# First attention with one exponential pass per four groups, and the change from feed-forward to second attention written out

## What is computed

```python
h = take_along(x, top_k(x @ w + b, 179))            # 179 of 256 tokens are kept
# layer 0: additive attention, 12 heads of 16
q, k, v = heads(ln(h) @ Wq.T + bq), heads(ln(h) @ Wk.T + bk), heads(ln(h) @ Wv.T + bv)
score = einsum('bhtsd,d->bhts', tanh(q[:, :, :, None, :] + k[:, :, None, :, :]), ws) + bs
h = h + (softmax(score) @ v) @ Wo.T + bo
h = h + quantized_ffn(ln(h))                         # 192 -> 768 -> 192, gelu
# layer 1: x is quantized with one scale for the whole tensor
xq = fake_quant(ln(h), scale = max(abs(ln(h))) / 127)
h = h + attention(xq)                                # power-of-two softmax
h = h + mixture_of_16_experts(ln(h))                 # one expert per token
```

## Time and profile before

| | |
|---|---|
| median of 3 runs | 1449.03 us (1444.05 to 1456.63) |
| the profiled execution | 1448.74 us, of which the span from first to last instruction is 1446.8 us |
| busy: PE, DVE, ACT, POOL | 1153.0, 1105.7, 1003.6, 861.9 us |
| DMA | 103.06 MB, most of it in the first 250 us |

### The profile page before, as it was taken

The page is one execution under the profiler, slowest core; times in us unless marked ns, Lnnn a source line. Parts: engine busy times, 40 slices in busy tenths (PEclk is TensorE's granted clock), DMA queues, the critical chain, the costliest instruction groups (busy, mean ns, idle before and its releaser), DMA issues. The chain is left out here.

```text
span 1446.8 us, 39002 instructions
## 1 busy us (share of the span) xinstructions
PE 1153.0 (80%) x16164; PEld 874.5 (60%) x16164; DVE 1105.7 (76%) x2109; ACT 1003.6 (69%) x921; POOL 861.9 (60%) x978
## 2 busy tenths in 40 slices
PE   4766898788778887887788779847999999989496
PEld 3544665566556655665566458835667666767396
DVE  8797998899889998998899867753566677665443
ACT  1389999999999999999999967732234433433142
POOL 4098878887888788888888977540012222123354
PEclk9899999999999999999999999975899999988698
DMA  9999997000000000000000002000000100010352
GB/s 254 360 360 356 352 344 246 2 2 2 2 2 2 2 2 2 2 3 2 1 2 2 2 15 53 0 1 1 2 2 12 59 17 15 12 39 9 94 152 65
DMA packets 75449, 103.06 MB, mean 71 GB/s; under 512 B 6303, under 2 KB 73640, under 8 KB 75282
## 3 DMA queue, kind: packets, MB, share of 16 engines
q1 hardware_dynamic: 63784, 87.90, 18.5%
q10 hardware_dynamic: 6860, 6.12, 1.6%
q0 software_dynamic: 4640, 6.65, 1.4%
HBM read 18.32 MB, written 83.85 MB: 71 GB/s over the span
## 5 line engine op out<-in xcount | busy, mean ns | idle before, releaser
L917 ACT ACTIVATE work<-work 128x2864 f32<-128x2864 f32 (+1 forms) x272 | 688.8, 2578 | 32.2 <-DVE work L436 31.3
L436 POOL TENSOR_TENSOR work<-shared 128x1253 f32<-128x1253 f32 (+1 forms) x272 | 613.5, 2267 | 151.6 <-PE psum L1789 117.8
L1789 PE MATMUL psum<-work,ws_place 128*32 128x179 f32 x8640 | 397.6, 325 | 165.8 <-ACT work L917 165.6
L436 DVE TENSOR_TENSOR work<-psum,shared 128x1611 f32<-128x1611 f32 (+3 forms) x288 | 486.5, 1722 | 0.6
L1789 PEld LDWEIGHTS psum<-work,ws_place 128*32 128x32 f32 x8640 | 261.7, 112 | 274.4 <-ACT work L917 214.2
L1979 PE MATMUL psum<-shared 32*64 32x179 f32 (+1 forms) x1728 | 142.5, 367 | 8.1 <-DVE shared L1497 8.1
L756 POOL TENSOR_TENSOR tsum<-tstats 128x4 f32<-128x4 f32 (+1 forms) x16 | 3.7, 233 | 200.8 <-DVE tstats L1414 200.8
L1276 DVE SCALAR_TENSOR_TENSOR p_sb<-psum,bs_col,s_top 128x358 f32<-128x358 f32 x144 | 82.1, 570 | 43.9 <-PE psum L1802 30.7
L1979 PEld LDWEIGHTS psum<-shared 32*64 32x64 f32 (+1 forms) x1728 | 81.1, 159 | 56.5 <-issue 36.5
L1503 DVE TENSOR_SCALAR pt_region<-pt_region 128x1074 uint32<-128x1074 uint32 x48 | 34.6, 721 | 98.4 <-ACT pt_region L988 98.4
L906 ACT ACTIVATE pt_region<-psum,bs_neg 128x512 f32<-128x512 f32 x144 | 95.3, 663 | 1.6 <-PE psum L1802 1.5
(11 more groups left out here) (365 smaller groups left out, 1984.2 us busy)
## 6 DMA issues: line engine op xcount, KB each, us to landing
xs_dram<-pad_row SPq DMA_DIRECT2D x23, 3088.0 KB, 27.6
pt_region<-xs_dram ACTq DMA_DIRECT2D x19, 193.0 KB, 2.6
pt_region<-xs_dram SPq DMA_DIRECT2D x19, 193.0 KB, 2.4
xs_dram<-pad_row SPq DMA_DIRECT2D x1, 2895.0 KB, 27.0
work<-in_x SPq DMA_DIRECT2D x2, 768.0 KB, 10.1
work<-in_x ACTq DMA_DIRECT2D x2, 768.0 KB, 16.2
work<-in_L_ffn_W2T SPq DMA_DIRECT2D x1, 1536.0 KB
work<-in_L_ffn_W1T SPq DMA_DIRECT2D x1, 1536.0 KB
```

The lines of the kernel that those rows point to most:

```text
L436: ins = eng.tensor_tensor(dst[:, a * KEEP:e * KEEP].rearrange("p (u s) -> p u s", s=KEEP), k[:, h * KP:h * KP + KEEP].unsqueeze(1).to_broa ...
L917: act.activation(a, a, ACT.Tanh).then_inc(tanh_done, 1)
L1789: ins = pe.matmul(bank_s[p % 2][32 * quad:32 * quad + 32, at:at + KEEP], ws_place[:, j, :], arg_slot(n)[:, u * KEEP:(u + 1) * KEEP], start ...
```

## The change

In the first attention `p_sb` holds the two groups of a duo 192 columns apart instead of 179, so 3 transposes of 128 take the place of 4 (2 for the last duo, as before). The three pieces are then: keys 0 to 127 of the even group; keys 128 to 178 of the even group and 0 to 63 of the odd group; keys 64 to 178 of the odd group. ACT takes the exponential of two banks, so of two duos (four groups), in one instruction of 128x768, after the tanh of groups 8, 12 and 16 and of groups 2 and (the single last group) 4 of the next batch: 5 passes a batch for 9. Duo k goes to bank k modulo 2, and PE may turn into it only once the pass over the pair before is done; duo 8 is turned at group 3 for group 2. Odd groups meet V in another order of rows, so SP copies V of each batch by three DMAs to `v_extra`, which PE waits for before the context; the context is made for even and odd groups apart, with 32 products of 96 columns and 32 of 48. SP issues two fills behind each batch's copies, until the 24 are out, instead of all at the start.

The last steps of DVE's feed-forward are written out: other order, the means of batches 14 and 15 by DVE and not POOL, with the additions of 14 and 15 ahead of them. The maximum over the partitions is a transpose on PE and a reduction on DVE. PE does 20 idle products instead of 12, not before `norm_max(12)` is done, and the transpose of the maximum stands behind them. The first batch's q, k and v go to four PSUM banks, without waits between. Two semaphores are merged into others, and two blanks are added on POOL at the start.

```diff
-        pt = [pt_region[:, 2 * n * PT_COLS:2 * (n + 1) * PT_COLS].rearrange("p (s c) -> p s c", s=2) for n in range(2)]
+        pt = [pt_region[:, 2 * n * PT_COLS:2 * n * PT_COLS + 3 * DUOS * 128].rearrange("p (s k c) -> p s k c", s=3, k=DUOS) for n in range(2)]
+        v_extra = [pt_region[:, 2 * n * PT_COLS + 3 * DUOS * 128:2 * n * PT_COLS + 3 * DUOS * 128 + 2 * HEADS * VC].rearrange(
+            "p (s h v) -> p s h v", s=2, h=HEADS) for n in range(2)]
...
-        p_sb = [sb(f"p_sb{n}", [128, KEEP + WIDE]) for n in range(2)]
+        p_sb = [sb(f"p_sb{n}", [128, 2 * ROW]) for n in range(2)]
...
+        def qkv_bank(c, fill):
+
+            if isinstance(c, int) and c == 0:
+                return (bank_pre, bank_out, bank_s1, bank_pta)[fill]
+            return bank_out if fill else bank_pre
+
...
-            for lo in range(0, XS_ROWS, 2048):
-                n = min(2048, XS_ROWS - lo) // 128
-                sp.dma_start(xs_dram[lo:lo + 128 * n, :].rearrange("(j p) d -> p j d", p=128),
-                             pad_row[:, :].unsqueeze(1).to_broadcast([128, n, RW])).then_inc(e_zeroed, 16)
+
+            def fill(n):
+
+                lo = 2048 * n
+                rows = min(2048, XS_ROWS - lo) // 128
+                sp.dma_start(xs_dram[lo:lo + 128 * rows, :].rearrange("(j p) d -> p j d", p=128),
+                             pad_row[:, :].unsqueeze(1).to_broadcast([128, rows, RW])).then_inc(e_zeroed, 16)
+
+            FILLS = -(-XS_ROWS // 2048)
+            for b in range(B):
+                n, v = b % 2, v_sb[b % 2]
+                sp.wait_ge(v_ready, b + 1)
+                need(sp, v_spread[n], 48 * (b // 2))
+                sp.dma_start(v_extra[n][HALF_K:128, 0, :, :], v[0:HALF_K, 0, :, :]).then_inc(v_spread[n], 16)
+                sp.dma_start(v_extra[n][0:HALF_K, 1, :, :], v[HALF_K:128, 0, :, :]).then_inc(v_spread[n], 16)
+                sp.dma_start(v_extra[n][HALF_K:LAST_K, 1, :, :], v[0:TB, 1, :, :]).then_inc(v_spread[n], 16)
+                for k in range(2 * b, min(2 * b + 2, FILLS)):
+                    fill(k)
...
-            with pool.Fori(0, B // 2) as j:
+            with pool.Fori(0, B // 2 - 1) as j:
                 pair_norms(j, 0)
-            pool.wait_ge(x_maxed, 1)
-            pool.partition_all_reduce(x_allmax[:, :], x_max[:, :], 128, RMAX).then_inc(x_alled, 1)
             pool.wait_ge(f_added, B)
...
-            def exps(b, k):
-
-                p, w = b * DUOS + k, duo(k)
-                if k == 0:
+            def exps(b, q):
+
+                if q == 0:
                     need(act, ctx_psum, 2 * b - 2)
-                act.wait_ge(turned, p + 1)
-                act.activation(pt[b % 2][:, :, 256 * k:256 * k + 128 * w],
-                               bank_pt[p % 2].rearrange("p (s c) -> p s c", s=2)[:, :, 0:128 * w],
-                               ACT.Exp, bias=bs_neg[:, :], scale=1.0).then_inc(exp_done, 1)
+                act.wait_ge(turned, b * DUOS + min(2 * q + 2, DUOS))
+                if q < EXPS - 1:
+                    banks = psum[:, 4 * 512:6 * 512].rearrange("p (k c) -> p k c", k=2)[:, :, 0:384].rearrange("p k (s c) -> p k s c", s=3)
+                    ins = act.activation(pt[b % 2][:, :, 2 * q:2 * q + 2, :].rearrange("p s k c -> p k s c"), banks,
+                                         ACT.Exp, bias=bs_neg[:, :], scale=1.0)
+                else:
+                    ins = act.activation(pt[b % 2][:, 0:2, 2 * q, :], bank_pta[:, 0:256].rearrange("p (s c) -> p s c", s=2),
+                                         ACT.Exp, bias=bs_neg[:, :], scale=1.0)
+                ins.then_inc(exp_done, 1)
             for b in range(B + 1):
...
-                    if g % 2 and g >= 7 and real(b):
-                        exps(b, (g - 7) // 2)
-                    if g in (0, 2, 3, 4) and real(b - 1):
-                        exps(b - 1, DUOS - 4 + (0, 2, 3, 4).index(g))
+                    if g in (8, 12, 16) and real(b):
+                        exps(b, (g - 8) // 4)
+                    if g in (2, 4) and real(b - 1):
+                        exps(b - 1, 2 + g // 2)
...
-                dve.scalar_tensor_tensor(p_sb[p % 2][:, 0:w * KEEP].rearrange("p (a s) -> p a s", s=KEEP), s, bs_col[:, :],
+                dve.scalar_tensor_tensor(p_sb[p % 2][:, 0:w * ROW].rearrange("p (a s) -> p a s", s=ROW)[:, :, 0:KEEP], s, bs_col[:, :],
...
+            def last_stats(n):
+
+                dve.wait_ge(f_added, B - 1 + n)
+                for t, rows in TILES:
+                    ins = dve.bn_stats(stats[0:rows, 2 + 2 * n + t, :], resid[0:rows, B - 1 + n, t, :])
+                rlink(ins)
...
+            def last_pair():
+
+                cols = slice(2, 6)
...
+                rlink(dve.tensor_tensor(v, vE, vO, ALU.add))
+                dve.tensor_scalar(m, m, 0.5, None, ALU.mult)
+                dve.tensor_scalar(v, v, 1.0 / D, EPS, ALU.mult, ALU.add)
+                rlink(dve.scalar_tensor_tensor(d, d, 0.25, d, ALU.mult, ALU.mult))
+                rlink(dve.tensor_tensor(v, v, d, ALU.add))
+                dve.tensor_scalar(h, v, -0.5, None, ALU.mult)
+                rlink(dve.tensor_copy(g, v.bitcast(I32)))
+                rlink(dve.tensor_scalar(g, g, -0.5, 1597463007.0, ALU.mult, ALU.add))
+                rlink(dve.tensor_copy(y.bitcast(I32), g))
+                for n in range(3):
+                    rlink(dve.tensor_tensor(s, y, y, ALU.mult))
+                    rlink(dve.tensor_tensor(s, s, h, ALU.mult))
+                    rlink(dve.scalar_tensor_tensor(y, s, 1.5, y, ALU.add, ALU.mult))
...
+            staged(dve, ffn_step, (2, 5), closed=True)
+            ffn_add(B - 4)
+            hidden_round(B - 3, 1)
+            dve.wait_ge(f_added, B - 3)
+            dve.wait_ge(stats_taken, B - 4)
+            pair_tile_stats(B - 3, 0)
+            norm_max(B - 7, 1)
+            ffn_add(B - 3)
+            hidden_round(B - 2, 0)
+            dve.wait_ge(f_added, B - 2)
+            pair_tile_stats(B - 2, 1)
+            norm_max(B - 6, 0)
+            norm_max(B - 5, 1)
+            ffn_add(B - 2)
+            hidden_round(B - 1, 1)
+            last_stats(0)
+            ffn_add(B - 1)
+            last_stats(1)
+            last_pair()
+            for b in range(B - 4, B):
+                norm_max(b, b % 2)
...
             dve.wait_ge(x_alled, 1)
+            dve.tensor_reduce(x_allmax[:, :], bank_k0[:, 0:128], AX.X, ALU.max).then_inc(x3_step, 1)
+            dve.wait_ge(x3_step, 1)
             dve.tensor_scalar(x_scale[:, :], x_allmax[:, :], 1.0 / 127.0, 1e-8, ALU.mult, ALU.max).then_inc(x3_step, 1)
...
-                bank, src = bank_pt[p % 2], p_sb[p % 2]
+                bank, src = bank_pt[k % 2], p_sb[p % 2]
                 pe.wait_ge(smax_done, p + 1)
-                need(pe, exp_done, p - 1)
-                for a in range(duo(k)):
-                    for s in range(2):
-                        ins = pe.transpose(bank[:, 256 * s + 128 * a:256 * s + 128 * a + 128],
-                                           src[:, a * KEEP + 128 * s:a * KEEP + 128 * s + 128], ident[:, :])
+                need(pe, exp_done, b * EXPS + k // 2)
+                for s in range(duo(k) + 1):
+                    ins = pe.transpose(bank[:, 128 * s:128 * s + 128], src[:, 128 * s:128 * s + 128], ident[:, :])
                 ins.then_inc(turned, 1)
-            def context(b, r, col):
-
-                first, second = (pt[b % 2][:, s, 0:PT_COLS // 32 * 32].rearrange("p (i c) -> p i c", c=32) for s in range(2))
+            def context(b, r):
+
+                n = b % 2
+                keys = [pt[n][:, s, :, :].rearrange("p k (i c) -> p k i c", c=32) for s in range(3)]
+                parts = [[(v_sb[n][:, 0, :, :], keys[0]), (v_sb[n][:, 1, :, :], keys[1])],
+                         [(v_extra[n][:, 0, :, :], keys[1]), (v_extra[n][:, 1, :, :], keys[2])]]
                 if r < 2:
-                    spans = [(0, UA // 4, 16 * r, col)]
+                    spans = [(KP * r, 16 * r, ((0, 6, 0), (0, 6, 16)))]
                 else:
-                    spans = [(UA // 4, PT_COLS // 32, 16 * n, col + UB * n) for n in range(2)]
-                for lo, hi, c, at in spans:
-                    for s, tile in ((0, first), (1, second)):
+                    spans = [(100 * m, 16 * m, ((6, 9, 16), (5, 8, 0))) for m in range(2)]
+                for at, c, groups in spans:
+                    for odd, (lo, hi, shift) in enumerate(groups):
                         for j in range(4):
-                            ins = pe.matmul(bank_out[32 * j:32 * j + 32, at:at + 4 * (hi - lo)].rearrange("p (i c) -> p i c", c=4),
-                                            v_sb[b % 2][:, s, 4 * r + j, :], tile[:, lo:hi, c + 4 * j:c + 4 * j + 4],
-                                            start=(s == 0), stop=(s == 1))
+                            cols = bank_out[32 * j:32 * j + 32, at + shift:at + shift + 32 * (hi - lo)].rearrange(
```

(34 more changed lines are left out.)

115 lines of the change are left out of this document (64 added, 51 removed).

## The result

The kernel after takes 1495.11 us (median of 4, 1493.03 to 1499.39) beside 1450.69 (median of 4, 1444.05 to 1456.63) before: ratio 1.0317, 95% interval 1.0267 to 1.0367. I had forecast 1466, with 1480 as the upper end. The direction was right, the size was not.

What follows compares the result with a forecast made beforehand. The prediction took a ring through ACT, PE and DVE, with ACT's steps on it, to bound the first attention. Its sum: 1448.74 + 21.2 - 0.5 + 1.5 + 1 - 5.6 = 1466.3 us, range 1444 to 1480.

Steps and rivals of the forecast that it cites:

- ACT's passes: First attention: four wide exponentials of 0.79 us replace eight of 0.57, saving ACT 1.40 us a batch (up to 1.60).
- The waits: First attention: ACT waits 1.69 us at group 2, 1.75 at group 8, 0.6 at group 16; batch 49.58 us.
- 14 x 1.41 - 0.5: First attention: a batch with one before it takes 1.41 us more; batch 0, without context, gains 0.5.
- In each stretch of half clock PE is later still and is now waited for: three stretches, 0 to 1.7 each, +1.5 together.: First attention: ACT waits for PE in three half-clock stretches, 0 to 1.7 us each, +1.5 us together.
- more falls of the clock: First attention: PE rests more around groups 0 to 4, falls cost 1 to 3 us each; 1480 us, chance 0.12.
- 8 x 1.8: First attention: one clock fall in half of the batches, at 1.8 us each, for a total of 1480 us.
- Moved without cost: First attention and token stage: V's copies, spread fills and POOL's blanks cost nothing; DVE loses nothing.
- Feed-forward to second attention: Transition: scale earlier by 3.7 us, two waits between q, k, v steps gone for 1.9; -5.6 us (-7.7 to -3.4).
- The clock at the start of the second attention, 0 taken: Second attention's start: PE comes warmer but DVE paces the first rounds; 0 us gained, with -12 as bound.
- the rival: Second attention starts at 2.4 GHz while the first attention's waits remain: 12 us less, 1454 us, chance 0.2.

Runs made afterwards that it cites:

- 6: Changed kernel plus 28 idle PE products in each batch of the first attention: 1469.79 us, ratio 1.015 to the kernel before.
- 3: Changed kernel plus 21 idle PE products in each batch of the first attention: 1482.53 us, ratio 1.017 to the kernel before.
- 9: Changed kernel with later exponentials and idle PE products in both attentions: 1422.72 us, ratio 0.973 to the kernel before.
- 8: Changed kernel with the scratch-row fills issued behind the last copy of V: 1500.31 us, ratio 1.036 to the kernel before.
- 5: Changed kernel with exponentials after groups 9, 13 and the next batch's 0, 2, 4: 1445.78 us, ratio 0.995 to the kernel before.
- 7: Changed kernel plus 8 idle PE products in the second attention's first batch: 1470.96 us, ratio 1.016 to the kernel before.

## Why the prediction was wrong, step by step

- *ACT's passes.* Right: from 592.54 to 593.33 are 0.79, as costed. But ACT's work in a batch fell by 1.15 (46.95 to 45.80) and not by 1.40: two neighbours overlap by 0.11, and each of the two new waits loses that.
- *The waits.* Right, a little high. Group 2: 1.70 for 1.69; group 8: 1.40 for 1.75, below its range of 1.50 to 2.08; group 16: 0.57 for 0.6; batch 49.47 for 49.58. That the batch fits so closely is in part luck: 0.35 less of waiting at group 8 and the 0.25 more of ACT's work nearly cancel. At group 8 the context grew by less than I took: 1.50 for the first part (553.07 to 554.57, before 1.34 from start to start) and 0.89 for the second (559.07 to 559.96, before 0.75), so 0.30 in all for the 0.65 taken (0.40 at least). The 64 records of 48 columns follow their columns, 13.9 ns from one to the next. By the floor of about 25 ns that the Trainium skill states (TensorE: Matmul & The Clock Gate, "Wait — 56ns, not 53.3ns?") they would have taken 1.60; the measurement decides against it for such products on four column groups. From the third tanh of batch 0 to that of batch 15 they cost 18.6 (6 against before without its 2.7 of falls). My terms for these intervals are 14 x 1.41 - 0.5 = 19.2.
- *"In each stretch of half clock PE is later still and is now waited for: three stretches, 0 to 1.7 each, +1.5 together."* This is the step that failed. I kept the number of falls of the trace before, and of those only the three that had made an interval longer. Seven fell within these intervals there, so even at that number the four that had cost nothing stood on what is now the awaited path. And the number did not stay: after it is 24, with falls in 14 of 15 batches (by the 0.84 at group 4). In place of +1.5 they cost 20.6 more than before (23.3 against 6, which has none, less before's 2.7). One wait was not in my list at all, 0.84 at group 4: the order puts the last turn of a batch at group 3, behind two score groups that are at half clock when it falls. That filling PE's rests takes the falls and their cost away is shown by 3, 6 and 9. That it was the longer rests that brought them is argued: rests of 1.84, 1.90 and 2.12 passed without a fall in the batch from 540.58. The rival "more falls of the clock" had the mechanism, with half the batches and a chance of 0.12; with 14 x 1.6 in place of its 8 x 1.8 it would have come to 1466 - 1.5 + 22.4 = 1487.
- *Moved without cost.* Right for fills and copies (8); no wait of PE for the copies of V is in the trace.
- *Feed-forward to second attention.* Right: -3.5 up to the first copy and 4.9 for 7.3 in the four steps, -5.9 together, for -5.6. The 20 idle products took 6.4 (5.9 to 8.5). The range of -7.7 to -3.4 did not follow from my own terms, which give -6.2 to -3.6. The feed-forward's own +3.6 was missing: a stretch at a lower clock that is in most, but not all, kernels with this transition and not in those with before's.
- *The clock at the start of the second attention, 0 taken.* Nearly right for the first four batches in sum (87.3 for 88.1, where the steps alone would have given 2.4 less), but for another reason: the first score rounds run at 2.4 GHz, as the rival had it, but behind one rest of 1.81 the half clock lasts 41 us. The +7.0 comes later and differs between two profiles of the same kernel, so what the change has to do with it is not shown.
- *In sum,* +47.7 between the profiles is 0.8 ahead of the first tanh (which came between 76.8 and 80.1 in these runs), 15.9 by waits and 23.3 by the clock in the first attention (18.6 and 20.6 if before's own falls are counted with the clock), 0.7 at its end, 3.6 in the feed-forward, -3.5 in the transition and 7.0 behind it.

## What to carry to other kernels

When a change lets PE or the engine that sets the pace wait longer, look in the trace for the rests that grow, and price a fall of the clock in each repetition, not as often as before. Count the falls before that cost nothing too: the change can put them on the path that is waited for. A merged pass saves its overhead only if its inputs are there when it is due: place it where the engine already waits, as in 5, and PE's lateness costs nothing. Take two profiles of the kernel before when its times spread: here the two differ by 14.7 us, 12.6 of it in one stage, where the clock fell for longer.

## What the runs showed of the hardware

- The granted clock fell to 0.50 behind rests of 2.38 (592.69), 1.91 (565.50 in 3) and 1.81 us (1032.33), but also behind two of 1.00 and 0.51 (1188.75), and it stayed at 1.00 over rests of 1.84, 1.90 and 2.12 in the batch from 540.58. The length of one rest did not decide it here.
- Idle products of 128 columns in PE's rests kept it at 1.00 from the third tanh of batch 0 to that of batch 15 (6), and for 290 us of the second attention (7).
- Once fallen it came back within some 7 us in the first attention (1.00 from about 599), but not for 41 us in the second, where PE was busy 9.0 to 10 of each 10 us from 1040 to 1070, and not for 51 us in another profile of the kernel before.
